# A three-stage decoder layer: layer-norm arithmetic moved from GpSimd to VectorE, one cast from ScalarE to GpSimd, one barrier left out

## The reference, cut to what matters

```
h = layernorm(x, g, b)
lin_out = linear_attention(h @ wq_lin + bq, h @ wk_lin + bk, h @ wv_lin + bv)
win_out = window_attention(h @ wq_loc + .., h @ wk_loc + .., h @ wv_loc + .., rel_bias)
gate = sigmoid(relu(concat[lin_out, win_out, h] @ wg1 + bg1) @ wg2 + bg2)
out = (gate * lin_out + (1 - gate) * win_out) @ wo + bo + x
x = layernorm(x + out)
```

## Time and profile before

| what | us |
|---|---|
| median of 3 runs (lowest, highest) | 700.94 (700.15, 704.07) |
| the profiled execution, its own time | 703.45 |
| span of its instructions | 701.6 |
| PE busy (share of the span) | 578.7 (82%) |
| DVE busy | 509.3 (73%) |
| ACT busy | 471.9 (67%) |
| POOL busy | 457.1 (65%) |

### The profile page before, as it was taken

One profiled execution on the slowest core, in us unless ns is written; L12 is line 12 of the kernel. 1 busy time (PEld: TensorE's weight loads), 2 busy tenths in 40 slices (PEclk: granted clock), 3 DMA queues, 4 the chain that ended last, 5 costly groups with the idle time before them and its releaser, 6 DMA issues.

```text
span 701.6 us, 24794 instructions
## 1 busy us (share of the span) xinstructions
PE 578.7 (82%) x8418; PEld 491.9 (70%) x8418; DVE 509.3 (73%) x2036; ACT 471.9 (67%) x1293; POOL 457.1 (65%) x623
## 2 busy tenths in 40 slices
PE   1789999999998756898878787856669999999393
PEld 1689999999897645665656565644569998889172
DVE  2898998998898324669999998555647776667283
ACT  3798999998998434667778776455227776666022
POOL 4746898999988851323767776453714777777583
PEclk9999999999999776979999999697699999999698
DMA  9410000002000002224455554322667656662394
GB/s 291 136 37 2 2 4 3 3 16 55 3 3 2 1 7 71 74 64 138 147 188 166 178 172 146 107 84 91 205 210 213 165 163 198 178 205 98 114 344 143
DMA packets 53644, 77.72 MB, mean 111 GB/s; under 512 B 8456, under 2 KB 42512, under 8 KB 52880
## 3 DMA queue, kind: packets, MB, share of 16 engines
q1 hardware_dynamic: 42768, 56.37, 27.2%
q0 software_dynamic: 7632, 16.87, 6.8%
q10 hardware_dynamic: 3120, 2.88, 1.2%
HBM read 48.49 MB, written 27.49 MB: 108 GB/s over the span
## 4 chain that ended last, share of the span: by engine, by line
PE 27%; DVE 18%; issue 9%; POOL 4%; ACT 3%; DMA 1%; DVEq 0%; ACTq 0%; POOLq 0%; SPq 0%
PE bank L2267 6%; DVE mnx L1526 4%; PE bank L2296 4%; PE bank L2236 3%; PE bank L2285 3%; PE bank L1751 3%; PE bank L1904 2%; DVE we_lo L1566 2%; PE bank L1823 1%; POOL ya L2086 1%; PE bank L1800 1%; DVE min_hl L1533 1%; PE bank L2277 1%; DVE min_hl L1535 1%; POOL frstd L2091 1%
## 5 line engine op out<-in xcount | busy, mean ns | idle before, releaser
L2078 POOL DMA_INDIRECT y_rows<-front,ix x95 | 94.0, 989 | 52.6 <-DVE ix L2182 31.5
L558 ACT ACTIVATE sc<-sc,mn 128x128 f32<-128x128 f32 x256 | 82.2, 410 | 2.4 <-DVE mn L770 2.4
L1375 POOL DMA_INDIRECT x_rows<-rows,slot_ix x64 | 65.1, 1018 | 16.3 <-issue 12.9
L2103 ACT ACTIVATE gT<-bank 128x512 f16<-128x512 f16 x95 | 56.4, 595 | 25.2 <-DVE eh_lo L2186 22.2
L770 DVE CUSTOM_DVE_ANT_0 sc<-bank,rel 128x128 f32<-128x128 f32 x256 | 57.7, 286 | 1.0 <-PE bank L902 0.7
L953 PE MATMUL bank<-hT,w_hi 128*128 128x128 f16 x512 | 52.7, 222 | 1.1 <-POOL hT L377 0.9
L565 ACT ACTIVATE pT_hi<-bank 128x512 f16<-128x512 f32 x64 | 38.4, 601 | 11.3 <-PE bank L912 10.9
L779 DVE TENSOR_TENSOR pT_lo<-bank,pT_hi 128x512 f16<-128x512 f32 x64 | 43.0, 673 | 1.0 <-ACT pT_hi L565 0.8
L2178 DVE COPY front<-bank 128x256 f32<-128x256 f32 x63 | 26.7, 424 | 22.8 <-PE bank L2296 22.2
L1526 DVE TENSOR_REDUCE mnx<-bank 128x4 f32<-128x512 f32 x64 | 39.6, 680 | 4.3 <-PE bank L1800 4.3
L912 PE MATMUL bank<-ident,sc 128*128 128x128 f32 x256 | 39.4, 276 | 0.5 <-DVE k_lo L760 0.5
(11 more groups left out here) (318 smaller groups left out, 2294.3 us busy)
## 6 DMA issues: line engine op xcount, KB each, us to landing
east<-in_experts SPq DMA_DIRECT2D x32, 384.0 KB, 3.4
hT<-x_rows SPq DMA_DIRECT2D x95, 129.0 KB, 2.5
rows<-xhl SPq DMA_DIRECT2D x16, 512.0 KB, 4.2
hT<-y_rows SPq DMA_DIRECT2D x16, 512.0 KB, 5.3
x_rows<-pad_block SPq DMA_DIRECT2D x32, 129.0 KB, 2.7
wst<-in_wcat SPq DMA_DIRECT2D x8, 256.0 KB, 6.6
front<-in_ctx_t SPq DMA_DIRECT2D x16, 128.0 KB, 2.8
out<-fin ACTq DMA_DIRECT2D x16, 128.0 KB, 5.2
```

Source lines behind the costliest of these rows:

```text
L558: done = act.activation(sc[:, g, j], sc[:, g, j], ACT.Exp, bias=mn[:, n % 2, g, j:j + 1], scale=-1.0)
L1375: pool.indirect_dma_start(shared.x_rows, bass.IndirectOffsetOnAxis(ap=slot_ix[:, n, k:k + 1], axis=0), rows4[:, q, k], None).then_inc(shar ...
L2078: pool.indirect_dma_start(c.y_rows, bass.IndirectOffsetOnAxis(ap=ix[:, n % IX], axis=0), yo[:, n % YO], None, bounds_check=NDEST - 1, oob_ ...
L2103: act.activation(gT[:, n % U], GT_BANK[n % len(GT_BANK)], ACT.Copy).then_inc(gt_r, 1)
```

## The change

`xn_` and `x1` are called on VectorE instead of GpSimd (`x1` is now named `x1_norm`); `lwhi` is called on GpSimd, in front of `lwlo`, instead of ScalarE; the barrier on L1120 goes. The waits inside the functions stay the same.

```diff
@@ gpsimd
+                    def lwhi(n):
+                        if live(n):
+                            pool.wait_ge(emptied["TT"], n + 1)
+                            wait(pool, filled["Z1"], n - 1)
+                            pool.tensor_copy(lwT_hi[:, n % 2], lwTf[:, n % 2]).then_inc(lwhi_r, 1)
+
-                    def xn_(n):
...
-                    def x1(n):
...
                     for i in range(NB + 8):
+                        lwhi(i - 6)
                         lwlo(i - 6)
                         hTlo(i - 2)
...
                         z1lo(i - 6)
-                        xn_(i)
                         vhi(i - 3)
                         vlo(i - 3)
-                        x1(i - 8)
                         ls(i - 6)
                         ld(i - 5)
@@ scalar
-                    def lwhi(n):
-                        if live(n):
-                            act.wait_ge(emptied["TT"], n + 1)
-                            wait(act, filled["Z1"], n - 1)
-                            act.activation(lwT_hi[:, n % 2], lwTf[:, n % 2], ACT.Copy).then_inc(lwhi_r, 1)
...
                         hThi(i - 1)
-                        lwhi(i - 5)
                         exps(i - 4, 3)
@@ vector
+                    def xn_(n):
+                        if live(n):
+                            s = n % 2
+                            dve.wait_ge(ln_rstd, n + 1)
+                            wait(dve, filled["T"], n - 1)
+                            dve.tensor_scalar(xn[:, s], xs[:, n], mv[:, s, 0:1], rstd[:, s], ALU.subtract, ALU.mult).then_inc(xn_ready, 1)
+
+                    def x1_norm(n):
+                        if live(n):
+                            s = n % 2
+                            dve.wait_ge(ln2_rstd, n + 1)
+                            dve.tensor_scalar(xs[:, n], yt[:, s], mv2[:, s, 0:1], rstd2[:, s], ALU.subtract, ALU.mult).then_inc(x1_ready, 1)
+
                         p_low(i - 5, 3)
                         kqr(i - 4)
+                        xn_(i)
                         kqb(i - 3)
                         lw0(i - 5)
                         rs(i - 5)
                         p_low(i - 4, 0)
                         lw1(i - 5)
+                        x1_norm(i - 8)
                         qlo(i - 2)
                         p_low(i - 4, 1)
@@ after the first block
-        nc.all_engine_barrier()
         nc.clear_and_free_semaphores(stage_sems[lasting:])
         nc.all_engine_barrier()
```

## The result

The changed kernel takes **704.84 us** (median of 22 runs, 698.19 to 709.48) against 700.92 for the kernel before beside it; the ratio is 1.0064, 95% interval 1.0039 to 1.0088, so it is 2.7 to 6.2 us slower. The profiled execution took 698.19 us, with a span of 696.4. That is less than the one before, so a single execution doesn't show the difference: the runs of either kernel scatter by over 1%. In this pair the change is hidden by the second and third stages, which no edit touches: from the first instruction of the second stage to the end it takes 440.1 us before (granted clock 0.90) and 431.9 here (0.93). What can be read exactly is the first stage, where the order of the work repeats to some hundredths of a microsecond.

A forecast was written before the change was run, and what follows sets the result against it. TensorE was taken as the bound of ordinary first-stage steps. Terms -1.92 + 2.8 + 0.35 - 0.9 + 0.3 - 0.35 gave +0.3 us, so 701.2 us against a median of 700.94; range 697.8 to 706.0.

The forecast's parts named there:

- rival A: First stage: x1_norm stands behind GpSimd's vloc_lo, scores late by 0.86 us a step, whole 707 us; chance 0.16.
- The bound and the place: First stage: TensorE bounds ordinary steps; scores, waiting on VectorE's last p_low, has only 0.07 us in hand.
- Rival B: First stage: the loop absorbs x1_norm's 0.28 us a step, so 2.8 goes out of the sum, 698.4 us; chance 0.19.
- C: Rival: only the stage's ends move; lwT_lo stays late in weight-piece steps, the loop has room, 700.3 us; chance 0.05.
- The weight-piece steps: Three first-stage steps with a GpSimd weight piece: lwT_lo comes 1.35 us earlier, three stretches of 0.64 go, -1.92 us.
- ten steps: Steps 8 to 17: x1_norm between lw1 and q_lo delays scores by about 0.28 us each, +2.8 us, bounds 0 and +10.
- let `x1_norm` go in front of `vloc_lo`: Near 121.8 us x1_norm was taken to start before GpSimd's vloc_lo, waiting only 0.08 us for the cast's remainder.
- `xn` hidden, cast hidden, `lwhi` off ScalarE worth nothing: First-stage steps: 0.65 us idle before kqb hides xn; GpSimd's step shortens despite the 0.65 cast; ScalarE's 0.63 saves nothing.
- Start: First stage's start: cast adds 0.65 us, xn brings the first transposition 0.9 earlier, 0.3 kept; sum +0.35.
- Later stages: Second and third stages should keep their times; more than 1 us difference would be a cause not known.
- End: First stage's end: last x1 on VectorE -0.9 us, x1_norm(13) before yt(14) +0.3, barrier gone -0.35.

The follow-up runs named there:

- b4: Kernel before with only xn moved to VectorE, in front of kqb: tiles 1 to 13 take 155.43 us against 157.22; whole 696.66 us, timed once.
- e3: Changed kernel with GpSimd's vhi, vlo and ls put in front of z1lo: ordinary steps 13.27 us against 13.73, ratio to the kernel before 1.0006.
- b5: Changed kernel with xn alone back on GpSimd, between z1lo and vhi: steps 13.26 us, tiles 1 to 13 158.97 us, one run.
- b1: Kernel before with only x1_norm moved to VectorE, behind lw1: steps 13.26 us, tiles 1 to 13 158.81 us against 157.22, one run.
- b2: Kernel before with only the barrier left out: last x1 to second stage 1.49 us instead of 1.80; tiles 1 to 13 157.19 us, one run.
- e5: Changed kernel with x1_norm one step later on VectorE, behind the next tile's yt and st2: ratio to the kernel before 0.9989.
- e6: As e5, with the cast lwhi also back on ScalarE: ordinary steps 13.49 us, ratio to the kernel before 0.9994.
- e4: Changed kernel with x1_norm right behind xn, in VectorE's idle time before kqb: ordinary steps 13.02 us, ratio to the kernel before 1.0014.
- e7: As e5, with GpSimd's vhi, vlo, ls before z1lo and the weight piece before ld: 692.29 us against 699.74, ratio 0.9895.

## Why the prediction was right and wrong

**The whole** came to +4.5 us by the ratio (2.7 to 6.2), where +0.3 was forecast. The time lies in the range, but between the forecast and rival A, and the range reached there because it was drawn to take in half of A: that the time falls into it is owed to the width of the range, not to the working. By the prediction's own half a per cent (3.5 us) the change is slower, to which it gave 0.17.

- *The bound and the place*: right. TensorE is the bound, the loop through the last `p_low` to `scores` has 0.07 to 0.08 us in hand, and what `x1_norm` puts into it comes out as step length; `scores` waits for `pT_lo` as foretold. Rival B (room in the loop) and C fell with it.
- *The weight-piece steps*, -1.92: right (b4 alone gives -1.79). Their waits for `lwT_lo` are gone, and they are 0.08 over the old 13.65 where the ordinary ones are 0.71 over 13.02.
- ***x1_norm* for ten steps, +2.8: the term that failed.** It measured 0.71 a step, +7.1. Its own length was near (0.40, against 0.35: e3 gives 0.25 a step). The step that failed is "let `x1_norm` go in front of `vloc_lo`". `x1_norm` did start first, 0.06 ahead (137.51 against 137.57) where the working had 0.09, and yet it ended 0.15 after `vloc_lo`; in b5 a lead of 0.10 was enough (last section). So rival A's mechanism decided, at 0.71 instead of 0.86 a step. I had weighed starts, and took the earlier start to win. So does the Trainium skill (SBUF — State Buffer, Who interferes with whom), by which whoever issues first gets the shared ports; a start 0.06 us ahead did not suffice here.
- *`xn` hidden, cast hidden, `lwhi` off ScalarE worth nothing*: right (b4; the cast 0.61 against 0.65). But I priced them apart from `x1_norm`, and b1 and b5 show the link: `xn` on GpSimd had kept `vloc_lo` out of its way.
- *Start*, +0.35: measured 49.42 - 49.59 = -0.17 from the first `bn_stats` to `lwTf` of tile 1. The cast cost 0.69 as said, and the first gate product waited 0.94 for `lwT_lo` instead of the 0.48 of the earlier trace rows; but the head start of `xn` was kept at 0.86, not 0.3.
- *Later stages*: said to keep their times within 1 us. In this pair of executions they differ by 8.2 us, with no edit there and another granted clock; the prediction had no term for the clock.
- *End*: the last `x1` -0.89 for -0.9, `yt(14)` 0.32 late for 0.3, the barrier -0.33 for -0.35 (b2: -0.31). The clock at the end of the stage, some -1.3 in this pair, was not in the sum either.

## What to carry to other kernels

Before an elementwise operation is moved to VectorE, look at what GpSimd does in that very moment once its own list has become shorter: not VectorE's free share, but its loop with the busiest engine and the neighbour's next instruction set the price. Move one piece at a time and read a stretch that repeats (a step at a constant clock); here one part of the change alone has the shorter stage, and the sum of the parts isn't the whole. When whole runs scatter by more than the change, that stretch tells what the total can't.

## What the runs showed of the hardware that I had not expected

- An `x1_norm` that meets a GpSimd `tensor_tensor` or cast (of 128x256 and more) ends 0.14 to 0.16 us after that instruction, and never sooner than 0.38 to 0.41 after its own start: `vloc_lo` (ends 138.23, `x1_norm` 138.38), `w_lo` in e5 (178.01, 178.15), `lwT_lo` in e6 (127.02, 127.16). An instruction of GpSimd that begins 0.09 us after it still goes first (`vloc_lo` at 219.62 in the changed kernel, 0.89 for `x1_norm`); one that begins 0.10 after it no longer does (218.98 in b5, 0.41). One that ends within its first 0.23 us costs it nothing (`vloc_lo` in e3, `lwT_hi` in e5).
- GpSimd's `tensor_scalar` with two operands per partition (1.23 us) let VectorE's pass in 0.40 (b1, b5), eight times out of eight in each.
- The granted clock fell to 0.50 at the end of the stage, once TensorE had gaps, for a time that differed from kernel to kernel; and to 0.83 in a stretch of ten microseconds of the fill in e4, e7 (40 to 50 us) and b5 (30 to 40 us), whose first tiles came late by as much as 2 us.
